# Counting edges: one-hot sets of four tiles in place of two, and region words of eight tiles in place of four

## What is computed

```python
edge_index = jnp.stack([src, dst])
x = x + _L0_gnn_ref(_layernorm(x), src, dst, ...)
x = x + _L0_ffn_ref(_layernorm(x)[None], ...)[0]
x = x + _L1_gnn_ref(_layernorm(x), edge_attr_4, edge_attr_8, edge_index, ...)
x = x + _L1_ffn_ref(_layernorm(x)[None], ...)[0]
```

```python
e = jnp.einsum('ehd,ehd->eh', k[src], q[dst]) / np.sqrt(DK).astype(np.float32)
m = jax.ops.segment_max(e, dst, num_segments=n)
ex = jnp.exp(e - m[dst])
z = jax.ops.segment_sum(ex, dst, num_segments=n)
attn = ex / z[dst]
a = jax.ops.segment_sum(attn[:, :, None] * v[src], dst, num_segments=n)
```

## Time and profile before

| | us |
|---|---|
| median of 3 runs | 1948.6 |
| lowest and highest run | 1948.49, 1955.6 |
| the profiled execution's own time | 1963.13 |
| its span in the trace | 1961.5 |
| count stage in it, first to last matmul | 240.7 to 386.6 |
| PE busy over the span | 1650.8 (84%) |
| DVE busy over the span | 987.2 (50%) |
| mean granted TensorE clock | 0.887 |

### The profile page before, as it was taken

How to read it: one execution, slowest core, us unless ns; L and a number is a source line. 1 busy time by engine, 2 the same in 40 slices (tenths; PEclk the granted TensorE clock), 3 DMA queues, 4 the chain that set the end, 5 groups by cost and what they waited for, 6 DMA issues and landing times. The chain is left out here.

```text
span 1961.5 us, 32798 instructions
## 1 busy us (share of the span) xinstructions
PE 1650.8 (84%) x9860; PEld 1173.8 (60%) x9861; DVE 987.2 (50%) x1998; ACT 696.4 (36%) x1609; POOL 557.6 (28%) x637
## 2 busy tenths in 40 slices
PE   1992067799999979689799999957999999897994
PEld 0540022288888845454799999944555555654663
DVE  8320256566667637635000000066999999632233
ACT  0220033255555513344212222124555555441331
POOL 6777500011101012215000000043555555133133
PEclk6996555599999989789899999966999999998997
DMA  6200280011010060065755655054555555528985
GB/s 172 59 7 7 60 334 0 10 23 22 11 21 11 1 153 1 24 222 143 287 191 215 242 196 189 9 169 142 156 155 159 152 155 155 190 61 273 333 267 178
DMA packets 131139, 252.81 MB, mean 129 GB/s; under 512 B 35344, under 2 KB 52596, under 8 KB 126572
## 3 DMA queue, kind: packets, MB, share of 16 engines
q1 hardware_dynamic: 91692, 171.81, 26.3%
q0 software_dynamic: 39360, 79.86, 14.3%
HBM read 196.03 MB, written 55.52 MB: 128 GB/s over the span
## 5 line engine op out<-in xcount | busy, mean ns | idle before, releaser
L2007 PE MATMUL acc<-prod,ohy 128*64 128x256 f32 x1056 | 249.1, 386 | 7.7 <-DVE prod L2122 7.7
L2051 ACT ACTIVATE ohy<-oh,RECS 128x64 f32<-128x64 f32 x704 | 187.0, 336 | 153.0 <-PE acc L2007 153.0
L2007 PEld LDWEIGHTS acc<-prod,ohy 128*64 128x64 f32 x1056 | 138.4, 138 | 132.8 <-issue 70.6
L686 PE MATMUL ps<-ohS,ohD 128*128 128x512 f16 x352 | 105.3, 460 | 124.3 <-DVE ohS L661 114.8
L1984 POOL DMA_INDIRECT rows<-up_dram,idx x176 | 166.9, 948 | 144.0 <-DVE prod L2122 100.9
L2010 PE MATMUL acc<-prod,ohy 128*64 128x256 f32 x704 | 177.4, 395 | 0.0
L267 POOL DMA_INDIRECT rec_dram<-recs,pos x157 | 160.3, 1021 | 59.8 <-issue 48.9
L1774 DVE TENSOR_SCALAR FT<-y_ps,b2T 128x188 f32<-128x188 f32 x32 | 13.2, 414 | 319.1 <-PE y_ps L1723 319.1
L1711 PE MATMUL hid_ps<-FT,W 128*128 128x188 f32 x1024 | 168.1, 326 | 0.7 <-ACT FT L1748 0.7
L2122 DVE TENSOR_TENSOR prod<-w_ps,rows 128x768 f32<-128x768 f32 x176 | 166.3, 945 | 0.0
L1711 PEld LDWEIGHTS hid_ps<-FT,W 128*128 128x128 f32 x1024 | 165.6, 192 | 0.9 <-issue 0.9
(11 more groups left out here) (381 smaller groups left out, 2675.5 us busy)
## 6 DMA issues: line engine op xcount, KB each, us to landing
W<-in_L_ffn_w SPq DMA_DIRECT2D x16, 4096.0 KB, 15.9
bankW_sp<-in_L_ffn_W_sp SPq DMA_DIRECT2D x2, 4096.0 KB, 24.9
xin<-zeros SPq DMA_DIRECT2D x31, 256.0 KB
h_dram<-h3e SPq DMA_DIRECT2D x22, 256.0 KB, 4.6
h<-h_dram SPq DMA_DIRECT2D x22, 256.0 KB, 2.7
QF<-q_dram SPq DMA_DIRECT2D x20, 250.0 KB, 4.2
xin_sp<-zeros SPq DMA_DIRECT2D x17, 256.0 KB
xin_fq<-zeros SPq DMA_DIRECT2D x17, 256.0 KB
```

Of the source, the lines that this page charges most:

```text
L686: last = nc.tensor.matmul(ps[:, bass.ds(region + c0, cn)], ohD[:, slot, :], ohS[:, slot, c0:c0 + cn], start=False, stop=False, skip_group_ ...
L2007: upper = lambda m: nc.tensor.matmul(acc[0:HALFB, bank, :].rearrange("p (b c) -> p b c", c=MUL)[:, m:4:3 - m, :], ohs[:, 1 + m, :], pr[:, ...
L2051: last = nc.scalar.activation(ohy[:, t % OHY, i, :], oh[:, par, t, :], ACT.Copy, scale=RECS[:, bass.ds(BATCH * g + t, 1), 4 + i])
```

## The change

DVE's and PE's unit becomes a set of four tiles, and a word holds the regions of eight tiles. The rings keep their eight tiles. So two sets are in flight, and a turn of PE's loop is one word and two sets; POOL grants by sets. In `front` the words are built from 176 numbers by seven multiply-adds in place of three, on 22 columns in place of 44.

```diff
-QUADS = -(-GROUPS // 4)
+WORD = 8
+WORDS = GROUPS // WORD
...
-                        for k in (2, 1, 0):
-                            step(nc.vector.scalar_tensor_tensor(out=quadI[:], in0=quadI[:], scalar=float(REGIONS), in1=in_quad[:, :, k],
+                        for k in reversed(range(WORD - 1)):
+                            step(nc.vector.scalar_tensor_tensor(out=wordI[:], in0=wordI[:], scalar=float(REGIONS), in1=in_word[:, :, k],
...
-            AHEAD, PAIRS = CRING // 2, GROUPS // 2
+            SET = WORD // 2
+            AHEAD, SETS = CRING // SET, GROUPS // SET
...
-                            turn = pool.value_load(turnI[0:1, bass.ds(2 * g + 2, 1)], min_val=1, max_val=BLOCKS)
+                            turn = pool.value_load(turnI[0:1, bass.ds(SET * g + SET, 1)], min_val=1, max_val=BLOCKS)
...
-                            dve.wait_ge(counted, n + 2)
-                            nc.vector.tensor_tensor(ohD[:, 2 * k:2 * (k + 1), :],
+                            dve.wait_ge(counted, n + SET)
+                            nc.vector.tensor_tensor(ohD[:, SET * k:SET * (k + 1), :],
...
-                            for t in range(2):
-                                last = nc.vector.tensor_scalar(ohS[:, 2 * k + t, :], nodes16[:], halfS[:, bass.ds(n + t, 1)],
+                            for t in range(SET):
+                                last = nc.vector.tensor_scalar(ohS[:, SET * k + t, :], nodes16[:], halfS[:, bass.ds(n + t, 1)],
...
-                            for t in range(2):
-                                slot = 2 * k + t
-                                region = region_in(regions, 2 * half + t) * REGION
+                            for t in range(SET):
+                                slot = SET * k + t
+                                region = region_in(regions, SET * half + t) * REGION
...
-                            last.then_inc(counted, 2)
-
-                        def regions_of(quad):
-                            return pe.value_load(quadI[0:1, bass.ds(quad, 1)], min_val=0, max_val=REGIONS ** 4 - 1)
-
-                        with pe.Fori(0, PAIRS // AHEAD) as r:
-                            for quad in range(AHEAD // 2):
-                                regions = regions_of(AHEAD // 2 * r + quad)
-                                for half in range(2):
-                                    sums(AHEAD * r + 2 * quad + half, 2 * quad + half, half, regions)
...
+                            last.then_inc(counted, SET)
+
+                        def regions_of(word):
+                            return pe.value_load(wordI[0:1, bass.ds(word, 1)], min_val=0, max_val=REGIONS ** WORD - 1)
+
+                        with pe.Fori(0, WORDS) as r:
+                            regions = regions_of(r)
+                            for half in range(2):
+                                sums(2 * r + half, half, half, regions)
```

More of the change, by code:

```diff
@@ L35 @@
 SLOTS = ETILES * LANES
-QUADS = -(-GROUPS // 4)
+WORD = 8
+WORDS = GROUPS // WORD
+assert WORDS * WORD == GROUPS and CRING == WORD
 EHID = 64
@@ L132, in gnn_moe_gnn_moe, with front @@
         low = sb("low", [128, GROUPS])
-        def front(KT, V, turnI, quadI, endI):
+        def front(KT, V, turnI, wordI, endI):
             with ExitStack() as st:
@@ L178, in front @@
                 odd, even = sb("odd", [LANES, GROUPS]), sb("even", [LANES, GROUPS])
-                region4 = sb("region4", [LANES, 4 * QUADS], I32)
+                region_of = sb("region_of", [LANES, GROUPS], I32)
                 fill = sb("fill", [LANES, ETILES // FILLS, REC])
@@ L358, in _ @@
                         step(nc.vector.tensor_scalar(turnI[:, 1:], blockI[:, 1:], 1.0, None, ALU.add))
[L359 to L362, removed]
-                        for k in (2, 1, 0):
-                            step(nc.vector.scalar_tensor_tensor(out=quadI[:], in0=quadI[:], scalar=float(REGIONS), in1=in_quad[:, :, k],
+                        step(nc.vector.memset(region_of[:], 0))
+                        step(nc.vector.tensor_scalar(region_of[:, 0:GROUPS], blockI[:, 1:], REGIONS - 1, None, ALU.bitwise_and))
+                        in_word = region_of[:].rearrange("p (q k) -> p q k", k=WORD)
+                        step(nc.vector.tensor_copy(wordI[:], in_word[:, :, WORD - 1]))
+                        for k in reversed(range(WORD - 1)):
+                            step(nc.vector.scalar_tensor_tensor(out=wordI[:], in0=wordI[:], scalar=float(REGIONS), in1=in_word[:, :, k],
                                                                 op0=ALU.mult, op1=ALU.add))
@@ L565, in query_tiles, with count_edges @@
             return QS, tiles_scored, q_split, stage, split
-        def count_edges(LA, stage, split, turnI, quadI, endI):
+        def count_edges(LA, stage, split, turnI, wordI, endI):
             HALFN = NODES // 2
             PARTS = [(0, 512), (512, HALFN - 512)]
-            AHEAD, PAIRS = CRING // 2, GROUPS // 2
+            SET = WORD // 2
+            AHEAD, SETS = CRING // SET, GROUPS // SET
             EARLY_ROUNDS = 4
@@ L575, in count_edges @@
                 RECS = sb("recs_in", [128, ETILES, REC])
-                PARTS_OF_RECS = ((0, 2 * AHEAD * EARLY_ROUNDS), (2 * AHEAD * EARLY_ROUNDS, ETILES))
+                PARTS_OF_RECS = ((0, SET * AHEAD * EARLY_ROUNDS), (SET * AHEAD * EARLY_ROUNDS, ETILES))
                 loaded = sems_in(st)("recs_loaded0", "recs_loaded1")
@@ L594, in groups @@
                         between()
-                    with engine.Fori(0 if between is None else EARLY_ROUNDS, PAIRS // AHEAD) as r:
+                    with engine.Fori(0 if between is None else EARLY_ROUNDS, SETS // AHEAD) as r:
                         for k in range(AHEAD):
                             body(AHEAD * r + k, k)
-                    for g in range(PAIRS // AHEAD * AHEAD, PAIRS):
+                    for g in range(SETS // AHEAD * AHEAD, SETS):
                         body(g, g % AHEAD)
@@ L651, in one_hots @@
                         def one_hots(g, k):
-                            n = 2 * g
+                            n = SET * g
                             dve.wait_ge(granted, g + 1)
                             dve.sem_inc(tick, 1)
-                            dve.wait_ge(counted, n + 2)
-                            nc.vector.tensor_tensor(ohD[:, 2 * k:2 * (k + 1), :],
-                                                    nodes16[:, 0:2 * HALFB].unsqueeze(1).to_broadcast([128, 2, 2 * HALFB]),
-                                                    key16[:, bass.ds(n, 2), :].rearrange("p a t -> p (a t)")
-                                                    .unsqueeze(2).to_broadcast([128, 2, 2 * HALFB]), ALU.is_equal)
-                            for t in range(2):
-                                last = nc.vector.tensor_scalar(ohS[:, 2 * k + t, :], nodes16[:], halfS[:, bass.ds(n + t, 1)],
+                            dve.wait_ge(counted, n + SET)
+                            nc.vector.tensor_tensor(ohD[:, SET * k:SET * (k + 1), :],
+                                                    nodes16[:, 0:2 * HALFB].unsqueeze(1).to_broadcast([128, SET, 2 * HALFB]),
+                                                    key16[:, bass.ds(n, SET), :].rearrange("p a t -> p (a t)")
+                                                    .unsqueeze(2).to_broadcast([128, SET, 2 * HALFB]), ALU.is_equal)
+                            for t in range(SET):
+                                last = nc.vector.tensor_scalar(ohS[:, SET * k + t, :], nodes16[:], halfS[:, bass.ds(n + t, 1)],
                                                                None, ALU.is_equal)
@@ L2716, in gnn_moe_gnn_moe @@
             KT, V = sb1("KT", [128, HEADS, NODES], F32R), sb1("V", [P, TILES, DIM])
-            turnI, quadI = sb1("turnI", [128, GROUPS + 1], I32), sb1("quadI", [128, QUADS], I32)
+            turnI, wordI = sb1("turnI", [128, GROUPS + 1], I32), sb1("wordI", [128, WORDS], I32)
             endI = sb1("endI", [128, BLOCKS], I32)
-            front(KT, V, turnI, quadI, endI)
+            front(KT, V, turnI, wordI, endI)
             LA = sb1("LA", [P, TILES, NODES])
             QS, tiles_scored, q_split, stage, split = query_tiles(attention)
-            count_edges(LA, stage, split, turnI, quadI, endI)
+            count_edges(LA, stage, split, turnI, wordI, endI)
             attend(KT, V, LA, FT, QS, tiles_scored, q_split, stage, split)
```

## The result

The change takes 1923.8 us (median of 4 runs, 1921.1 to 1926.5) against 1951.5 us of before beside it: a ratio of 0.9857, with a 95% interval of 0.983 to 0.9884. That is 27.6 us less, where 25.7 were forecast. On a second occasion the ratio was 0.9879 (0.9859 to 0.99), 24.9 us between the medians. Each interval reaches some 5 us to either side, so the runs confirm the direction and the rough size; the terms of the sum are checked in the traces. Faster was right, and the time is in the range.

What follows compares the result with a forecast made beforehand. PE's sequencer, loading words and branching, was taken to bound the count stage. Terms 27.1 + 2.2 - 0.9 - 0.2 - 2.5 = 25.7 us gained took the median from 1948.6 to 1922.9 us, range 1914 to 1936.

Steps and rivals of the forecast that it cites:

- PE's turn: PE's count loop: eight tiles take 5.14 us in place of 6.37, over 22 turns 27.1 us gained.
- The long loads: Word loads while DMA writes zeros cost 0.56 us extra each; fewer loads pay it, 2.2 us gained.
- The first set: Start of the count stage: PE waits for four tiles' one-hots in place of two's, 0.9 us lost.
- The last set: End of the count stage: a set of four may keep PE's array busy for 2.39 us, 0.2 us lost.
- The second keys: DVE in the count stage: they delay its next set by 1.98 us, covered by idle time, costing nothing.
- The ring: Two sets between DVE and PE: round trip 4.90 us against a 5.14 us turn, 0.24 to spare, costing nothing.
- at most the 2.39 us of a quad with a seam in it: The time for PE's set of four tiles, used in the 4.90 us round trip of a slot.
- POOL's split: POOL splits the first query tile late in the count stage, slowing DVE: 2.5 us lost, bounds 0 to 3.2.
- PE's clock rises: Rival: denser turns lift PE's granted clock, up to some 3 us off attention's first scores; 1920 us, chance 0.2.
- Both ring rivals: Two-set ring binds partly, 1928 to 1938 us, chance 0.1; or makes the kernel slower, 1962 us, chance 0.04.
- the hidden gain: Rival: the stage also ends with the zeros in HBM, so nothing shows; 1948 us, chance 0.04.
- PE's gaps did not follow the end of `ohS` by 0.4 us: Sign of being wrong: such gaps between sets in every turn would make the ring the bound.

Runs made afterwards that it cites:

- Experiments 1: Words of eight tiles, but DVE and PE still work by pairs, four in the ring, against the kernel before: ratio 0.9906.
- 2: Sets of four tiles, two in the ring, but a word of four tiles before each, against the kernel before: ratio 0.9956.
- 4: Words of twelve tiles and a ring of three sets of four, against the kernel before: 1915.1 us, ratio 0.9819.
- experiment 5: The changed kernel with PE's loop unrolled to 24 tiles a turn, first with two sets in the ring, then three: ratios to before 0.9834 and 0.9838.
- Experiment 7: SP's zero fills moved from the count stage behind attention's loads, in the change and in the kernel before: ratios to before 0.984 and 0.9973.
- Experiment 6: Both kernels of experiment 5 with one more DVE instruction in each set: ratios to before 0.9851 with two sets in the ring, 0.9837 with three.
- the last kernel: Words of twelve tiles, two a turn, three sets in the ring, zero fills moved, against the kernel before: 1910.9 us, ratio 0.9791.

## Why the prediction was right

- **PE's turn, 27.1 us.** The traces show turns of 5.17 and 5.20 us where 5.14 was reckoned, so the term is 22 x (6.37 - 5.19) = 26.0 us. The excess is within the sets, where tiles follow at 0.44 to 0.52 us. Experiments 1, 2, 4 and 5 move the seams and give back their prices, the larger sets alone least exactly.
- **The long loads, 2.2 us.** Experiment 7 puts their cost at 6.5 us before and 3.3 us after, so 3.2 were gained. I had given each a fixed 0.56 us; what is left costs 3.3 / 8 = 0.41.
- **The first set, 0.9 us lost.** From DVE's first instruction to PE's first matmul it is 2.26 us (239.62 to 241.88) against 1.44 before (239.26 to 240.70): 0.8 us. *The last set* cost nothing: its last tile ends 0.6 us behind its weight load, before 0.8 us.
- **The second keys, nothing.** They pushed DVE's next set back by 1.99 us (259.71 to 261.70), and its `ohS` were still done 0.91 us before PE's first matmul, where 0.4 is the least.
- **The ring, nothing.** Right in the result, and too cautious in the margin. The step "at most the 2.39 us of a quad with a seam in it" is what was too long: sets take 1.8 us where the clock is up and up to 2.3 where it is not, and the build 1.86 for 1.94. With these the round trip is 4.2 or 4.7 us (1.8 or 2.3, then 0.14 + 1.86 + 0.40), and the margin 1.0 or 0.5 us in place of 0.24. Part of it is thus owed to the clock, which the forecast had at 0.50. Experiment 6 shows that 0.33 us more a set still fit.
- **POOL's split, 2.5 us lost.** The place and the mechanism were right, the size was too large:

```profile
333.64 1.25 DVE L664 TENSOR_SCALAR ohS<-nodes,halfS 128x625 f16<-128x625 f16 x4
...
333.79 1.81 PE L689 MATMUL ps<-ohS,ohD 128*128 128x512 f16 x8 [0.90 <-issue]
...
335.84 1.82 PE L689 MATMUL ps<-ohS,ohD 128*128 128x512 f16 x8 [0.25 <-issue]
...
336.34 3.98 DVE L664 TENSOR_SCALAR ohS<-nodes,halfS 128x625 f16<-128x625 f16 x4
...
336.91 1.02 POOL L560 CAST QS<-QF 128x1000 fp32r<-128x1000 f32 x1 [102.45 <-issue]
...
338.02 2.12 POOL L562 TENSOR_TENSOR QS<-QF,QS 128x1000 fp32r<-128x1000 f32 x1
340.24 0.68 DVE L659 TENSOR_TENSOR ohD<-nodes,key 128x512 f16<-128x512 f16 x1
...
340.71 4.35 PE L689 MATMUL ps<-ohS,ohD 128*128 128x512 f16 x16 [3.05 <-DVE ohS L664]
```

PE's sets start 340.71 - 335.84 = 4.87 us apart where 3.11 is usual over word and branch (304.76 to 307.87 above), so 1.76 us were lost. The four `ohS` took 3.98 us for 1.25, hence DVE was held 2.7 us, and the margin of the ring took a microsecond of it. The Trainium skill states the lock (SBUF — State Buffer, "SBUF: two separate sides"), and this trace agrees: DVE is held for most of POOL's 3.1 us, and its next `ohD` starts 0.1 us after POOL's second instruction ends (338.02 + 2.12 = 340.14). The trace of before agrees too. I had read there that the `ohS` beside the CAST "did finish", but they took twice their usual 0.67 us:

```profile
361.60 1.44 DVE L661 TENSOR_SCALAR ohS<-nodes,halfS 128x625 f16<-128x625 f16 x2
```

The 3.1 us lost that I had worked out from the lock missed the margin above all (1.0 us for 0.24), not the rule.
- **The sum.** 26.0 + 3.2 - 0.8 - 1.8 = 26.6 us by the trace (attention's first scores come 26.2 us earlier), 25.7 forecast, 27.6 and 24.9 in the runs. That it comes so close is in part luck: the turn gave 1.1 us less than reckoned, the long loads 1.0 and POOL's split 0.7 more.
- **The rivals.** *PE's clock rises* did occur, though I had given it 0.2: from 0.50 to 0.68 and 0.79. Its 1920 us and the forecast's 1922.9 are too close for the runs to tell apart; the traces show the rival's clock and the forecast's gain. As I had argued, the turn did not care, and at attention's start the first scores took 1.68 us for 2.44, but the clock was down again for most of its first 8 us, so of the 3 us at most one was had. The Trainium skill (TensorE: Matmul & The Clock Gate, Part 1) states that sustained activity releases the throttled clock. The trace agrees: a turn at 1.2 GHz keeps PE busy for 84% now (4.35 of 5.19 us), the steady stretch of before for 75%. But a stretch with 82% had stayed at 0.50, so what decides is not shown here. The higher level was of no use to a stage held by PE's sequencer, but for the ring's margin. Both ring rivals and the hidden gain are excluded. PE's gaps did not follow the end of `ohS` by 0.4 us: in a steady set it is 335.84 - (333.64 + 1.25) = 0.95 us, and only the first set and the one at POOL's split come to 0.4. And the runs moved by 1.4%.

## What to carry to other kernels

Before blaming the engine that the trace names as releaser, list an engine's start-to-start times over one turn of its loop and see which instruction stands at each long one. Here the long ones stood at a word read from memory and at a branch, and a table of four seam prices, with the long loads and the split beside it, foretold the stage of the longer words, of the words of twelve, of the longer turn and of the last kernel to about 1 us, and that of the larger sets alone to 2. A ring may then be made shallower as long as its round trip, with the slowest set and the slowest build, stays under the new turn; look for the one place where another engine holds the builder up.

## What the runs showed of the hardware that I had not expected

- A word's load by the sequencer took 0.30 us, and up to 1.04 us while DMA wrote 376 GB/s; the same instructions with the fills moved away took at most 0.50.
- TensorE's granted clock was 0.79 in the steady part of the stage, a mix of both levels, and the loop's turns there were alike to 0.1 us but for the one at POOL's split.
- On the second chip the kernel before took 2040.8 us in place of 1951.2. Some 78 us of the 90 lie before the first count (319.4 us in the first kernel of experiment 5, 241.9 in the change), in the front, whose projections no kernel here changes. PE issued most matmuls of the projections one every 2.80 us there, from 91 to 235 us, in that kernel's timeline:

```profile
158.62 0.54 PE L418 MATMUL ps<-FT,Wqkv 128*128 128x226 f32 x1 [2.26 <-issue]
161.42 0.54 PE L418 MATMUL ps<-FT,Wqkv 128*128 128x226 f32 x1 [2.26 <-issue]
```

Which part of the chip holds it there stays open. The ratios of that chip are against its own longer time, which moves them by less than 0.001.
